# A three-layer CIN kernel: x turned by TensorE, one running sum over all of d, two layers ended together, and another start

## What is computed

```python
x: (512, 39, 32)            # b, field, d
hidden = x
for i in range(3):
    z = einsum('bmd,bnd->bmnd', x, hidden).reshape(B, -1, D)
    cur = relu(einsum('bcd,co->bod', z, W[i]) + b[i])      # 200 outputs
    if i < 2: hidden, direct = cur[:, :100], cur[:, 100:]
    else:     direct = cur
    finals.append(direct)
y = sum over d of concatenate(finals, axis=1)              # (512, 400)
```

## Time and profile before

| | |
|---|---|
| median of 3 runs | 2790.56 us (2789.16 to 2792.14) |
| profiled execution | 2791.72 us, its span 2790.0 us |
| PE busy | 2702.3 us, 97% |
| DVE busy | 2667.3 us, 96% |
| ACT busy | 1698.4 us, 61% |
| DMA, mean over the span | 120 GB/s |

### The profile page before, as it was taken

How to read it: one execution, slowest core, us unless ns; L and a number is a source line. 1 busy time by engine, 2 the same in 40 slices (tenths; PEclk the granted TensorE clock), 3 DMA queues, 4 the chain that set the end, 5 groups by cost and what they waited for, 6 DMA issues and landing times.

```text
span 2790.0 us, 56206 instructions
## 1 busy us (share of the span) xinstructions
PE 2702.3 (97%) x18112; PEld 2661.2 (95%) x18112; DVE 2667.3 (96%) x3218; ACT 1698.4 (61%) x3179; POOL 1.2 (0%) x11
## 2 busy tenths in 40 slices
PE   1799999999999999999999999999999999999999
PEld 1799999999999999999999999999999999999998
DVE  3799999999999999999999999999999999999997
ACT  2566666666666666666666666666666666666664
POOL 0000000000000000000000000000000000000000
PEclk9999999999999999999999999999999999999999
DMA  8454544454554454454454454445444445444541
GB/s 194 109 128 110 129 122 108 120 133 108 125 128 109 114 139 109 115 131 115 108 136 117 109 128 124 108 125 128 108 121 122 118 116 132 112 111 123 127 108 59
DMA packets 346786, 333.97 MB, mean 120 GB/s; under 512 B 151970, under 2 KB 281614, under 8 KB 346638
## 3 DMA queue, kind: packets, MB, share of 16 engines
q1 hardware_dynamic: 346762, 333.67, 48.0%
HBM read 332.73 MB, written 8.37 MB: 122 GB/s over the span
## 4 chain that ended last, share of the span: by engine, by line
PE 82%; DVE 8%; issue 4%; DMA 3%; ACT 2%; SPq 1%; DVEq 0%; ACTq 0%
PE acc L659 51%; PE acc L660 24%; PE acc L647 5%; DVE z_low L384 4%; DVE z L380 2%; DMA xb<-x_by_unit 1%; PE summed L677 1%; PE turned L671 1%; ACT z_high L525 1%; DMA xb<-in_L_rec_b_dram 1%; DVE z L361 1%; ACT hid L544 0%; DMA w_rows_again<-in_L_rec_W_dram 0%; DMA xb<-in_L_rec_W_dram 0%; DVE w_split L349 0%
## 5 line engine op out<-in xcount | busy, mean ns | idle before, releaser
L659 PE MATMUL acc<-w_split,z_high 128*128 128x400 f32 (+1 forms) x8320 | 2511.8, 369 | 64.6 <-DVE z_low L384 58.5
L660 PE MATMUL acc<-w_split,z_low 128*128 128x200 f32 (+1 forms) x8320 | 2120.5, 255 | 0.0
L525 ACT ACTIVATE z_high<-z 128x1024 fp32r<-128x1024 f32 (+3 forms) x1152 | 1125.0, 977 | 882.4 <-DVE z L380 728.3
L659 PEld LDWEIGHTS acc<-w_split,z_high 128*128 128x128 f32 (+1 forms) x8320 | 1565.4, 188 | 88.5 <-issue 78.4
L660 PEld LDWEIGHTS acc<-w_split,z_low 128*128 128x128 f32 (+1 forms) x8320 | 1593.0, 191 | 0.0
L384 DVE TENSOR_TENSOR z_low<-z,z_high 128x1024 fp32r<-128x1024 f32 (+3 forms) x1152 | 1282.5, 1113 | 45.3 <-ACT z_high L525 45.0
L380 DVE TENSOR_TENSOR z<-hid,xb 128x1024 f32<-128x1024 f32 (+2 forms) x1024 | 1142.0, 1115 | 11.2 <-DMA xb<-x_by_unit 10.9
L544 ACT ACTIVATE hid<-turned 32x128 f32<-32x128 f32 x768 | 205.3, 267 | 8.9
L541 ACT ACTIVATE hid<-turned 96x512 f32<-96x512 f32 x256 | 150.4, 588 | 91.8 <-PE turned L671 91.6
L647 PE MATMUL acc<-w_whole,z_whole 128*128 128x200 f32 x1024 | 197.7, 336 | 3.1 <-DVE s L391 3.1
L647 PEld LDWEIGHTS acc<-w_whole,z_whole 128*128 128x128 f32 x1024 | 168.9, 190 | 3.4 <-DVE s L391 3.4
(11 more groups left out here) (25 smaller groups left out, 72.0 us busy)
## 6 DMA issues: line engine op xcount, KB each, us to landing
xb<-x_by_unit SPq DMA_DIRECT2D x384, 384.0 KB, 4.4
x_right<-x_by_unit SPq DMA_DIRECT2D x384, 136.5 KB
xb<-x_by_unit SPq DMA_DIRECT2D x384, 128.0 KB, 5.0
xb<-x_by_unit SPq DMA_DIRECT2D x128, 336.0 KB
xb<-x_by_unit SPq DMA_DIRECT2D x128, 84.0 KB
x_left<-x_by_unit SPq DMA_DIRECT2D x384, 19.5 KB
xb<-in_L_rec_W_dram SPq DMA_DIRECT2D x6, 600.0 KB, 9.4
x_by_unit<-in_r_x_dram SPq DMA_DIRECT2D x128, 19.5 KB
```

Source lines behind the costliest of these rows:

```text
L525: nc.scalar.activation(z_high[slot][0:rows, 0:n * T], z[slot][0:rows, 0:n * T], ACT.Copy).then_inc(high, 1)
L659: nc.tensor.matmul(a[:, 0:2 * O], z_high[slot][0:rows, tok], w, start=(c == 0), stop=False, skip_group_check=True)
L660: last = nc.tensor.matmul(a[:, 0:O], z_low[slot][0:rows, tok], w[:, 0:O], start=False, stop=(c == chunks - 1), skip_group_check=True)
```

## The change

A unit is now 128 values of b at one value of d: 4 tiles of 128 rows of x, with 32 units each.

- x: SP loads a tile of 128 rows, PE turns it in 10 blocks (`turn_x`), ACT copies it from PSUM (`turned_x`), SP stores it to the same scratch in DRAM. For the tiles after the first this lies in the period d = 4 of the tile before.
- Sum over d: it is now one running sum over 32 units in `direct` [128, 4, 100]. The matmuls that summed columns, ACT's copies behind them and `o_row` are gone. SP stores `direct` itself. There is one `add` over all three layers per unit.
- Layers 0 (of unit n+2) and 1 (of unit n) are ended together, with one instruction of each kind at twice the width: one `second_half`, one `sums`, one `dup`, two transposes back to back, one `hidden`. Before they were ended apart. The place of both transposes is behind group 0 of the next period, and `hidden` stands between the roundings of groups 1 and 2.
- The 4 unsplit chunks of layer 2 are gone; it has 31 chunks split like the others.
- Prologue: less of W0 is copied within DRAM, the first x goes through PE, and the split of W2 moves out of the prologue into unit 0 and period 1, between their products.
- Loops: 5 units at the head of each tile are written out, then a loop takes two units a round, where it took four.

```diff
-            def hidden(l, u, par):
-                h = hid[l + 1][par]
-                act.wait_ge(turned_in[l], u + 1)
-                nc.scalar.activation(h[0:MAIN, :, :], turned[l][0:MAIN, 0:T].unsqueeze(1).to_broadcast([MAIN, GROUPS, T]), ACT.Relu)
-                nc.scalar.activation(h[MAIN:P, GROUPS - 1, :], turned[l][MAIN:P, 0:T], ACT.Relu)
+            def hidden(a, b, step, par):
+                h, t = hid[par][:, a:b, :, :], turned[:, 0, 0:2 * P].rearrange("p (l t) -> p l t", t=P)[:, a:b, :]
+                act.wait_ge(turned_in, step)
+                nc.scalar.activation(h[0:MAIN, :, :, :], t[0:MAIN, :, :].unsqueeze(2).to_broadcast([MAIN, b - a, GROUPS, T]), ACT.Relu)
+                nc.scalar.activation(h[MAIN:P, :, GROUPS - 1, :], t[MAIN:P, :, :], ACT.Relu)
                 for g in range(GROUPS - 1):
-                    last = nc.scalar.activation(h[MAIN:P, g, :], turned[l][32 * g:32 * (g + 1), 0:T], ACT.Relu)
+                    last = nc.scalar.activation(h[MAIN:P, :, g, :], t[32 * g:32 * (g + 1), :, :], ACT.Relu)
...
@@ ACT, period
                 highs(base, slot(0), P, group_chunks(0))
-                if before0:
-                    dup(0, n + 1)
+                    dup(a1, 2, ended(n - 1))
                 highs(base + 1, slot(1), P, group_chunks(1))
-                hidden(1, n - 1, 1 - par)
+                    hidden(a1, 2, ended(n - 1), 1 - par)
                 highs(base + 2, slot(2), P, group_chunks(2))
...
                 highs(base + 3, slot(3), P, group_chunks(3))
-                if before0:
-                    hidden(0, n + 1, 1 - par)
...
@@ PE, period
                 multiply(1, base, slot(0), 0)
-                if before0:
-                    transpose(0, n + 1)
+                    transpose(a1, 2, ended(n - 1))
                 multiply(1, base + 1, slot(1), 1)
...
-                multiply_whole(n - 1, 1 - j % 2)
...
                 multiply(2, base + q + 3, slot(q + 3), 3)
-                transpose(1, n)
...
@@ PE, new
+            def turn_x(r):
+                pe.wait_ge(x_in, 32 * (r + 1))
...
+                for k in range(BLOCKS):
+                    bank, j = k // X_PER_BANK, k % X_PER_BANK
+                    t = nc.tensor.transpose(x_turned[:, bank, j * T:(j + 1) * T], x_tile(r)[:, k * P:(k + 1) * P], ident)
...
@@ DVE
+            def add(a, b):
+                return nc.vector.scalar_tensor_tensor(direct[:, a:b, :], s[:, a:b, 1, 0:HID], 0.0, direct[:, a:b, :], ALU.max, ALU.add)
...
+                if not second:
+                    sums2(n - 2)
+                directs(r, d, n)
...
+                if second:
+                    low_piece(8, 2, 3)
```

More of the change, by code:

```diff
@@ L29 @@
 XROWS = F + SHIFTS * L0_CHUNKS - 1
+NEAR = 13
+REST = F - NEAR
+WRAP = 20
+Q = 4
+BLOCKS = 10
+FIELDS = Q * BLOCKS
+WRAP_BLOCKS = 5
+X_BANKS = 3
+X_PER_BANK = 4
+X_STORES = 2 * Q
 MAIN = 96
@@ L75, in first, with ended, layers_ended @@
     return PERIOD * n - 2
+def ended(n):
+    return n + 3
+def layers_ended(r, d):
+    return (1, 2) if r == TILES - 1 and d >= D - 2 else (0, 2)
 def cin_kernel(nc, r_x, W0, W1, W2, b0, b1, b2, out):
@@ L145, in cin_kernel @@
         freed = sem("freed")
[L146 to L153, removed]
+        half_in, half2_in = sem("half_in"), sem("half2_in")
@@ L231, in _, with load_w0 @@
-            sp.wait_ge(xt_done, 32)
+            def load_w0(near):
+                f0, n = (0, NEAR) if near else (NEAR, REST)
+                cols, rows = (w0, w0) if near else (w0c_t, w0r_t)
+                per_col, per_row = (F, F) if near else (REST + WRAP, REST)
+                for k in range(SHIFTS):
+                    last = len(range(k, L0_PAIRS, SHIFTS))
+                    at = slice(k * F + f0, k * F + f0 + n)
+                    sp.dma_start(pair_w[at, 0:last, :],
+                                 bass.AP(cols, k * O, [[(per_col + 1) * O, n], [SHIFTS * O, last], [1, O]])).then_inc(pairs_w_in, 16)
+                    c = 1 if k == 0 else 0
+                    sp.dma_start(pair_w2[at, c:last, :],
+                                 bass.AP(rows, (k + SHIFTS * c) * per_row * O,
+                                         [[(per_row + 1) * O, n], [SHIFTS * per_row * O, last - c], [1, O]])).then_inc(pairs_w_in, 16)
@@ L237, in _ @@
[L237 to L251, removed]
+            sp.wait_ge(ones_set, 1)
+            for g in range(2):
+                load_w(sp, 1, g, W1, b1)
+                load_xb(0, 0, g)
             sp.wait_ge(product, 1)
             load_pairs(1)
[L254 to L262, removed]
@@ L394, in directs, with sums @@
[L394 to L405 removed]
+            def sums(a, b, step, added):
+                dve.wait_ge(half_in, step)
+                if added is not None:
+                    dve.wait_ge(direct_in, added)
+                nc.vector.tensor_tensor(s[:, a:b, :, 0:HID], acc[:, a:b, 0:O].rearrange("p l (h o) -> p l h o", o=HID),
+                                        half[:, a:b, :, :], ALU.add).then_inc(s_in, 1)
@@ L555, in _, with high_piece @@
+            def high_piece(l, g):
+                act.wait_ge(w_in[GROUPS * (l - 1) + g], W_COUNT[g])
+                high_w(piece(l, g), stage(l, g))
+            for bank in range(X_BANKS):
+                turned_x(0, bank)
             act.wait_ge(pair_sum, 1)
@@ L579, in _, with period @@
                 highs(at + g, slot_of(at + g), P, group_chunks(g))
+                if g == 1:
+                    hidden(0, 1, 2, 1)
             highs(at + GROUPS, slot_of(at + GROUPS), L0_ROWS, L0_CHUNKS)
-            second_half(1, 0, at + 3)
-            second_half(0, 2, at + 4)
-            dup(1, 0)
-            def period(m, j, base, sl, layer0=True, before0=True, before2=True):
-                n, par = m * QUARTERS + j, j % 2
+            high_piece(2, 0)
+            def period(r, d, n, base, sl):
+                par = d % 2
+                second, final = (r, d) == (0, 1), (r, d) == (TILES - 1, D - 1)
+                turn = d == HEAD - 1 and r < TILES - 1
+                a, b = layers_ended(r, d)
+                a1 = 1 if final else 0
                 def slot(p):
@@ L617, in period @@
-                if before2 and j == 1:
-                    results(2, m - 1)
-                highs(base + q + 3, slot(q + 3), P, split_chunks(2, 3))
-                dup(1, n)
-            period(0, 1, first(1), first(1) % RING, before2=False)
-            period(0, 2, first(2), first(2) % RING)
-            period(0, 3, first(3), first(3) % RING)
-            with act.Fori(0, UNITS // QUARTERS - 2) as i:
-                for j in range(QUARTERS):
-                    period(i + 1, j, first(i * QUARTERS + (QUARTERS + j)), first(j + QUARTERS) % RING)
@@ L628, in _ @@
-            last = UNITS // QUARTERS - 1
-            for j in range(QUARTERS):
-                n = last * QUARTERS + j
-                period(last, j, first(n), first(n) % RING, layer0=j < 2, before0=j < 3)
+                if second:
+                    high_piece(2, 3)
+                if turn:
+                    turned_x(r + 1, 1)
+                highs(base + q, slot(q), P, group_chunks(0))
+                if turn:
+                    turned_x(r + 1, 2)
+                highs(base + q + 1, slot(q + 1), P, group_chunks(1))
@@ new lines, in period @@
+                if final:
+                    second_half(a, b, base + q - 1)
+                highs(base + q + 2, slot(q + 2), P, group_chunks(2))
+                if final:
+                    dup(a, b, ended(n))
+                else:
+                    second_half(a, b, base + q - 1)
+                highs(base + q + 3, slot(q + 3), P, group_chunks(3))
+            for r in range(TILES):
+                for d in range(1 if r == 0 else 0, HEAD):
+                    n = r * D + d
+                    period(r, d, n, first(n), slot_of(first(n)))
+                with act.Fori(0, (loop_end(r) - HEAD) // 2) as i:
+                    for j in range(2):
+                        period(r, HEAD + j, i * 2 + (r * D + HEAD + j), first(i * 2 + (r * D + HEAD + j)), slot_of(first(HEAD)))
+                for d in range(loop_end(r), D):
+                    n = r * D + d
+                    period(r, d, n, first(n), slot_of(first(n)))
@@ L642, in _ @@
         @block.tensor
         def _(pe):
-            def multiply_whole(u, par):
-                pe.wait_ge(whole, u + 1)
-                for c in range(WHOLE):
-                    last = nc.tensor.matmul(acc[2][:, 0:O], z_whole[par][:, c * T:(c + 1) * T], w_whole[:, c, :], start=(c == 0), stop=False,
-                                            skip_group_check=True)
-                last.then_inc(whole_used, 1)
             def multiply(layer, number, slot, g=0):
-                c0, n = (0, L0_CHUNKS) if layer == 0 else (GROUP * g + split_from(layer, g), split_chunks(layer, g))
+                c0, n = (0, L0_CHUNKS) if layer == 0 else (GROUP * g, group_chunks(g))
@@ L724, in period @@
```

(17 more changed lines are left out.)

660 lines of the change are left out of this document (336 added, 324 removed).

## The result

The changed kernel takes 3318.34 us (3307.45 to 3338.49, 4 runs) against 2790.25 us: a ratio of 1.190, 95% interval 1.185 to 1.195. I had forecast 3238, with a range to 3310. The direction and the mechanism were right, and the time lies 80 us above the forecast and 8 above the range.

What follows compares the result with a forecast made beforehand. DVE's 20.92 us plus 3.52 idle behind ACT's hidden layers made 24.44 a period. Start 104, 124 periods, a 22.4 period, end 46, x 3 and clock 37 gave 3243, rounded to 3238 us; range 3150 to 3310.

Steps and rivals of the forecast that it cites:

- What bounds: Before the change, DVE's work nearly fills the period; turn, hidden, round, subtract is about as long as its covering work.
- DVE's own work, 20.92: DVE's instructions per period after the change: 20.63 us plus 0.29 for wider operations and the split of layer 2.
- PE's own work: PE's 69 pairs and two transposes take at most 20.8 us a period, fitting into DVE's period.
- The chain, 24.44 a period: Group 0's z_low to group 2's takes 7.93 us against 4.41 of DVE work; 3.52 idle added to 20.92.
- The clock: PE's 2.97 us idle ahead of group 2 lowers its clock in half the periods: +37 us, bounds 0 and 93.
- periods of 26: Rival: the clock's fall reaches group 0, whose 8 pairs take 2 us more inside the chain; 3450 us; 7% beyond range.
- Prologue: W2's split moves out of the start, gaining 17 us (0 to 19); period 2 begins near 104 instead of 120.92.
- End and x: After the last period 46 us (43 to 48); turning x for three later tiles adds 3 us (0 to 9).
- The sum: Start, periods, end, turning x and clock add to 3243 us for the kernel, 3244 for its profiled execution.
- the small gain that I had rounded in: Fewer waits for DMA, up to 11 us, taken as likely and rounded in: 3243 became 3238 us.
- The range: 3150 us (no clock fall, shorter chain, better prologue) to 3310 (a fall each period, worse prologue), at 81%.
- The rival on the faster side: `hid` does not hold up group 2, so DVE's 20.92 us is the period: 2760 us, 1.1% faster; chance 3%.

Runs made afterwards that it cites:

- e1: The changed kernel with ACT's hidden-layer instructions moved from ahead of group 2's rounding to behind group 3's; 2795.91 us, ratio 1.0024 to the kernel before the change.
- e3: The changed kernel with both of PE's transposes put ahead of group 0's pairs instead of behind them, ACT's order unchanged; 2904.02 us.
- e5: Kernel e1 with the running sum `direct` on DVE moved behind layer 0's next product; 2766.49 us, ratio 0.9918 to the kernel before the change.
- e2: The changed kernel with 12 matmuls whose results nobody uses added on PE behind group 1 in each period; 3223.99 us.
- e8: Kernel e6 with ACT splitting W2's third piece ahead of the hidden layers in period 1 alone; 2728.44 us, ratio 0.978 to the kernel before the change.
- e6: Kernel e5 with layer 2's 4 unsplit chunks restored, using one product buffer instead of two; 2730.89 us, ratio 0.979 to the kernel before the change.
- e7: The changed kernel with 4 unused matmuls on PE behind group 1 in each period, instead of the 12 of e2; 3247.25 us.
- e4: The changed kernel with the four 32-partition hid instructions moved behind group 2's rounding, only the 96-partition one staying ahead of it; 3110.76 us.

## Why the prediction was right in kind and short in size

- **What bounds.** Right. The 0.42 us of the earlier trace rows was the end of a chain that had been just covered, and the change stretched it. e1 takes it away with ACT's order alone, and e3 most of it with PE's order alone.
- **DVE's own work, 20.92.** 0.18 too low: 21.10 in e1, since `direct` waits for the sum ahead of it, and 20.88 once that is cured (e5).
- **PE's own work** doesn't bind: right, e1 has a period set by DVE.
- **The chain, 24.44 a period.** Right, and a little by luck. Periods without a fall of the clock are 24.51, but DVE's own part of it is 0.18 longer and the wait 0.12 shorter (3.40, not 3.52) than I had them. e2 gives 3224 in all, against 3206 and 1.7 for the sum without the clock.
- **The clock.** This is the step that failed, by its size. I put 37 us into the sum, for falls of 3.4 us in half of the periods, and bounded it at 93 us by a fall in each, with 0.6 to 0.75 for each. e2 shows the measured size: without the falls the kernel is 94 us faster (88 us by the periods of the profiled executions). So my upper bound was the measured value, but by other numbers: a fall of 3.4 us costs only 0.4 (PE's slack takes more than I gave it), and a fall can last 6.8 us, which I had not considered. A long one costs 1.75, as PE then comes late to the next group 0, which stands in the chain. Among the rivals I had periods of 26, but for a fall that lasts into group 0. The long fall shown ends at 2750.8, some 12 us before group 0; what reaches it is PE's lateness. (The 3450 us of that rival belong to a period of 26.4; at 26 they would be 3400.) The likeliest value should have been at the upper end, since the rows of before showed a fall behind both of the waits I had and no wait that passed without one. The expected 2.97 us of idleness was 2.67, and that was enough.
- **Prologue.** Period 2 begins at 112.22 and not at 104, 8 us late. In period 1 DVE waited 8.50 us for W2's third piece, and that was mostly no transfer but the same chain again: on ACT the piece stands behind hid, which waited 4.33 us for PE's transposes. e8 shows it: with the piece ahead of hid, the wait is 1.5, and period 2 begins at 104.
- **End and x.** The end is 46.5 us (46). Turning x for the next tile shows as 0.5 us over the quiet period in e2, 1.5 in all (3).
- **The sum.** The profiled execution is 71 us over my 3244. The clock makes 51 of them (88 for 37), the prologue 8, and 124 periods of 24.54 instead of 24.44 make 12, of which 3 stood in the sum already, for turning x; 3 are left. The other 9 of the 80 are the small gain that I had rounded in, which didn't come, and 3 us by which the median of the four runs lies over the profiled one.
- **The range** ended at 3310, worked out from falls in each period and a bad prologue; the first cost what I had bounded it at, the second came, and the small gain that I had rounded in did not.
- **The rival on the faster side** needed the chain to be covered. It was not in this kernel, but it is what e1 makes of it, with 2796 us where I had 2760: 0.18 a period from `direct` are 22 of the 36, and 9 are from the prologue.

One reading of the rows was wrong. The row at 120.92 in the earlier trace rows is the product of group 1 in period 2. The product of group 0, the place that 112.22 here and 2747.21 in the earlier trace rows stand for, is this one in the kernel before:

```profile
118.62 1.22 DVE L380 TENSOR_TENSOR z<-hid,xb 128x1024 f32<-128x1024 f32 x1
```

So the period before was 21.03 and not 21.01, which changes nothing, and the start gained 6.4 us where I forecast 17.

What stays open: why some falls last 6.8 us. All 38 long ones begin 0.5 to 0.8 us before PE resumes its pairs at group 2. The short ones begin from 0.1 us before that moment to 1.6 behind it, but for the first and the last. This is only seen beside each other in one execution, and no run was made to move the one and watch the other.

## What to carry to other kernels

Merging small instructions saves busy time on the engine: one `hid` at twice the width takes ACT 2.59 us where before it took 1.74 for each of the two layers. But it also makes everything wait for the later of the merged steps and puts the sum of their lengths in front of what is queued behind. Here DVE was to save 0.2 us a period and lost 3.4. The greater part of the loss is a matter of place: 2.5 go with PE's transposes ahead of group 0 (e3), and the other 0.9 with `hid` behind group 3 (e1). What decides is which instruction stands behind the merged one, and how much other work lies between the start and the end of the chain. No run has the narrow instructions at the new place, so what the width alone costs is not shown. With the chain's parts placed well (e1), `direct` moved (e5) and the old treatment of the four chunks (e6), the changed kernel with its other savings is 2% faster than the kernel before.

A wait of under 1 us in a tuned loop is worth following to its root before the order is changed: it tells which chain is just covered.

## What the hardware did that I had not expected

- Adding 2.36 us of useless matmuls to each period made the kernel 94 us faster (3318 to 3224), because the granted clock stayed at 1.00.
- An idle time of 1.92 us (e7) in a loop of 24.5 still let the clock fall to 1.2 GHz in some periods. Two of 0.99 and 1.18 us, 3.8 us apart in a loop of 23.6 (e4), did not, though together they are longer.
- With PE idle for 2.67 us in each period, falls came twice in four periods for 1100 us and then in nearly each, in one and the same execution. The runs of this kernel scatter by 1% (3307 to 3338), where e2's scatter by 0.1%.
